# First tile of a time-mix and expert kernel: T1 to exponential in two halves, small constants on GpSimd, fourth tile's statistics in two pieces

## The reference, cut to what matters

```
xn  = layernorm(x);  xn1 = layernorm(xn) * ln1_g + ln1_b
r   = sigmoid(xn1 Wr');  w = -exp(xn1 Ww');  k = xn1 Wk';  v = xn1 Wv'
e   = exp(w + k);  decay = exp(time_decay)
num = decay*num + e*v;  den = decay*den + e      (a scan over the tokens)
a   = xn + (r * num / (den + 1e-8)) Wo'
a   = a + sigmoid(an Wrec') * (relu(an Wkey')^2 Wval'),   an = layernorm(a)*ln2_g + ln2_b
x2  = x + a
out = x2 + shared_ffn(h) + expert_ffn(h * score),   h = layernorm(x2), one expert of 16 per token
```

## Time and profile before

| what | value |
| --- | --- |
| median of 3 runs | 484.36 us (484.09 to 484.52) |
| the profiled execution's own time | 484.58 us |
| its span | 482.9 us |
| PE busy | 472.7 us (98%) |
| DVE busy | 371.4 us (77%) |
| POOL busy | 352.6 us (73%) |
| ACT busy | 324.2 us (67%) |
| moved by DMA | 39.32 MB, mean 81 GB/s |
| chain that ended last, by engine | PE 84%, DVE 6%, issue 3%, DMA 2%, ACT 2%, POOL 2% |

### The profile page before, as it was taken

How to read it: one execution, slowest core, us unless ns; L and a number is a source line. 1 busy time by engine, 2 the same in 40 slices (tenths; PEclk the granted TensorE clock), 3 DMA queues, 4 the chain that set the end, 5 groups by cost and what they waited for, 6 DMA issues and landing times.

```text
span 482.9 us, 10368 instructions
## 1 busy us (share of the span) xinstructions
PE 472.7 (98%) x3025; PEld 383.6 (79%) x3025; DVE 371.4 (77%) x1076; ACT 324.2 (67%) x625; POOL 352.6 (73%) x571
## 2 busy tenths in 40 slices
PE   8999999999999999999999999999999999999997
PEld 7556677868777778686777868877889999999996
DVE  7899899999999999996899989847545455555426
ACT  2777887987978879777687986563265555565421
POOL 6667498898898988986798877767326777767750
PEclk9999999999999999999999999999999999999999
DMA  7052001102102011010101001011489855542028
GB/s 240 2 191 115 1 23 44 56 12 67 34 33 68 23 45 56 12 66 24 44 24 46 33 12 46 33 42 39 121 187 246 229 167 150 150 130 72 23 68 282
DMA packets 33031, 39.32 MB, mean 81 GB/s; under 512 B 4913, under 2 KB 29113, under 8 KB 32720
## 3 DMA queue, kind: packets, MB, share of 16 engines
q1 hardware_dynamic: 26640, 24.98, 18.1%
q0 software_dynamic: 5760, 13.16, 7.8%
q10 hardware_dynamic: 576, 0.52, 0.3%
HBM read 21.69 MB, written 17.93 MB: 82 GB/s over the span
## 4 chain that ended last, share of the span: by engine, by line
PE 84%; DVE 6%; issue 3%; DMA 2%; ACT 2%; POOL 2%; SPq 1%; DVEq 0%; POOLq 0%; ACTq 0%
PE bank L442 20%; PE bank L435 11%; PE bank L459 6%; PE bank L450 4%; PE bank L850 4%; PE bank L858 3%; PE bank L857 3%; PE bank L548 3%; PE bank L560 3%; PE bank L544 3%; PE bank L539 3%; PE bank L429 3%; PE bank L534 2%; PE bank L605 2%; PE bank L619 2%
## 5 line engine op out<-in xcount | busy, mean ns | idle before, releaser
L442 PE MATMUL bank<-hT,wm 128*128 128x256 f32 x512 | 124.7, 383 | 0.6 <-ACT kr L974 0.6
L442 PEld LDWEIGHTS bank<-hT,wm 128*128 128x128 f32 x512 | 92.0, 190 | 18.7 <-issue 8.5
L1630 POOL DMA_INDIRECT sorted_rows<-rows,posi x64 | 72.8, 1138 | 20.1 <-issue 16.9
L1725 POOL DMA_INDIRECT out<-shared x55 | 53.2, 967 | 36.2 <-DVE shared L1542 22.7
L435 PEld LDWEIGHTS bank<-wm,k 128*128 128x128 f32 x512 | 61.7, 192 | 8.0 <-issue 6.4
L435 PE MATMUL bank<-wm,k 128*128 128x128 f32 x512 | 62.4, 275 | 0.1
L1153 ACT ACTIVATE er<-bank 128x256 f32<-128x256 f32 x40 | 15.3, 383 | 41.6 <-PE bank L858 40.9
L1550 DVE TENSOR_TENSOR e<-er,bank 128x256 f32<-128x256 f32 x40 | 16.8, 421 | 22.5 <-ACT er L1153 18.9
L459 PE MATMUL bank<-wm,actA 128*128 128x128 f32 x240 | 32.9, 280 | 0.0
L1010 ACT ACTIVATE h<-rows,smE 128x128 f32<-128x128 f32 x64 | 26.3, 482 | 8.1 <-POOL smE L1606 8.0
L459 PEld LDWEIGHTS bank<-wm,actA 128*128 128x128 f32 x240 | 29.3, 192 | 0.2 <-issue 0.2
(11 more groups left out here) (267 smaller groups left out, 1289.5 us busy)
## 6 DMA issues: line engine op xcount, KB each, us to landing
shared<-sorted_rows SPq DMA_DIRECT2D x56, 128.5 KB, 3.4
shared<-x SPq DMA_DIRECT2D x16, 256.0 KB, 2.8
rows<-sorted_rows SPq DMA_DIRECT2D x24, 128.5 KB, 2.4
wexp<-w_exp SPq DMA_DIRECT2D x2, 1536.0 KB, 8.6
sorted_rows<-filler SPq DMA_DIRECT2D x17, 128.5 KB
shared<-out SPq DMA_DIRECT2D x6, 256.0 KB
out<-shared SPq DMA_DIRECT2D x12, 128.0 KB, 2.2
sorted_rows<-rows,posi POOLq DMA_INDIRECT x64
```

The costliest lines, as they stand in the source:

```text
L442: ins = mm(dst[:, j * HALF:(j + 1) * HALF], W(name, 2 * pair_ + j), src[:, half * HALF:(half + 1) * HALF], start=True, stop=True)
L1630: g_.indirect_dma_start(sorted_ap, bass.IndirectOffsetOnAxis(posi[t % 3][:, g:g + 1].bitcast(U32), 0), rows[t % 3][:, g, :], None).then_in ...
L1725: g_.indirect_dma_start(out, bass.IndirectOffsetOnAxis(xr[k % RING][:, j, D:D + 1].bitcast(U32), 0), xr[k % RING][:, j, D + 1:ROW], None, ...
```

## The change

- Tile 0 goes from the transposes to the exponential in two halves of 256 tokens. PE transposes groups 0 and 1 into T1_B and groups 2 and 3 into T2_B, each half with its own wait. The Ww and Wk products are issued half by half (W, K, W, K), each half into a bank of its own. ACT copies, and takes both exponentials, half by half, and DVE subtracts half by half. The semaphores T1, xn1T, Wp, Kp, ew, z and e now count two for each tile; other tiles raise them by two at once.
- In the normalisation of tile 0, DVE now does groups 0, 1 and 3 (with a signal of its own behind group 1) and ACT group 2.
- `consts` and `rev_const` leave DVE. POOL does them right behind `col_no`, ahead of the powers of tile 0: five memsets, then `region0`, `region`, `part_row0`, `part_eid` and four pieces of `rev`. DVE waits for them (`const_p` at 8) behind the second piece of the statistics.
- The statistics of tile 3 leave the place ahead of DVE's rounds. Their first piece (`spread_of_x`, four BATCH_NORM_STATS2) stands between the two half subtractions, the second (`mean_of_x`, four BATCH_NORM_AGGREGATE) behind them.

```diff
-    agA=2, pA=3, xn1tok=1, xn0=1, T1=1, xn1T=1, Wp=1, Kp=1, Rp=1, Vp=1, ew=1, z=1, e=1, er1=2, ev=1,
+    agA=2, pA=3, xn1tok=1, xn0=1, T1=2, xn1T=2, Wp=2, Kp=2, Rp=1, Vp=1, ew=2, z=2, e=2, er1=2, ev=1,
...
+T1_of, W_of, K_of = (T1_B, T2_B), (W_B[:, 0:HALF], SMALL[:, 0:HALF]), (K_B[:, 0:HALF], T2_B[:, 0:HALF])
...
-HALF_TILE = 5
+HALF_TILE, CONSTS_P, ACT_GROUP = 5, 8, 2
...
     def transposes(dst, src, done):
...
-        ins.then_inc(s[done], 1)
+        ins.then_inc(s[done], PER[done])
...
-        if t == 0:
-            pe.wait_ge(s["const_d"], HALF_TILE)
...
+    def first_turn():
+        for half in range(2):
+            pe.wait_ge(s["const_d"], HALF_TILE + half)
+            if half:
+                wait(pe, "xn1tok", 0)
+            for g in range(2 * half, 2 * half + 2):
+                ins = nc.tensor.transpose(grp(T1_of[half], g), grp(xn1tok[0], g), ident[:, :])
+            ins.then_inc(s["T1"], 1)
+    def first_products():
+        pe.wait_ge(s["w_in0"], 16)
+        for half in range(2):
+            tokens = xn1T[0][:, half * HALF:(half + 1) * HALF]
+            wait(pe, "xn1T", 0, half + 1)
+            mm(W_of[half], W("Ww"), tokens, start=True, stop=True).then_inc(s["Wp"], 1)
+            mm(K_of[half], W("Wk"), tokens, start=True, stop=True).then_inc(s["Kp"], 1)
     def w_product(t):
-        pe.wait_ge(s["xn1T"], t + 1)
-        if t == 0:
-            pe.wait_ge(s["w_in0"], 16)
+        pe.wait_ge(s["xn1T"], 2 * (t + 1))
...
-        mm(W_B[:, :], W("Ww"), xn1T[t % 2][:, :], start=True, stop=True).then_inc(s["Wp"], 1)
+        mm(W_B[:, :], W("Ww"), xn1T[t % 2][:, :], start=True, stop=True).then_inc(s["Wp"], 2)
     def r_product(t):
-        pe.wait_ge(s["xn1T"], t + 1)
+        pe.wait_ge(s["xn1T"], 2 * (t + 1))
...
-            if t != 2:
+            if t == 0:
+                first_turn()
+            elif t != 2:
...
-            if t != 2:
+            if t == 0:
+                first_products()
+            elif t != 2:
...
+            if t == 0:
+                continue
...
-            mm(K_B[:, :], W("Wk"), xn1T[t % 2][:, :], start=True, stop=True).then_inc(s["Kp"], 1)
+            mm(K_B[:, :], W("Wk"), xn1T[t % 2][:, :], start=True, stop=True).then_inc(s["Kp"], 2)
...
     def norm_x(t):
...
-        for g in range(G if t else 1):
+        for g in range(G) if t else [ACT_GROUP]:
...
     def copy_x(t):
-        act_e.wait_ge(s["T1"], t + 1)
-        af(xn1T[t % 2][:, :], T1_B[:, :], ACT.Identity, bias=V("b1"), scale=V("g1")).then_inc(s["xn1T"], 1)
+        if t == 0:
+            for half in range(2):
+                part = slice(half * HALF, (half + 1) * HALF)
+                wait(act_e, "T1", t, half + 1)
+                af(xn1T[0][:, part], T1_of[half][:, part], ACT.Identity, bias=V("b1"), scale=V("g1")).then_inc(s["xn1T"], 1)
+            return
+        act_e.wait_ge(s["T1"], 2 * (t + 1))
+        af(xn1T[t % 2][:, :], T1_B[:, :], ACT.Identity, bias=V("b1"), scale=V("g1")).then_inc(s["xn1T"], 2)
...
     def exp_z(t):
+        if t == 0:
+            for half in range(2):
+                part = slice(half * HALF, (half + 1) * HALF)
+                wait(act_e, "z", t, half + 1)
+                af(e[0][:, part], ew[0][:, part], ACT.Exp).then_inc(s["e"], 1)
+            return
...
-        af(e[t % 2][:, :], ew[t % 2][:, :], ACT.Exp).then_inc(s["e"], 1)
+        af(e[t % 2][:, :], ew[t % 2][:, :], ACT.Exp).then_inc(s["e"], 2)
...
     def exp_w(t):
+        if t == 0:
+            for half in range(2):
+                wait(act_e, "Wp", t, half + 1)
+                af(ew[0][:, half * HALF:(half + 1) * HALF], W_of[half], ACT.Exp).then_inc(s["ew"], 1)
+            return
...
-        af(ew[t % 2][:, :], W_B[:, :], ACT.Exp).then_inc(s["ew"], 1)
+        af(ew[t % 2][:, :], W_B[:, :], ACT.Exp).then_inc(s["ew"], 2)
...
-    def consts():
-        for j in range(PACK):
-            ins = v.memset(place16[:, :, j], float(NE ** j))
-        const(ins)
-        dve.wait_ge(s["const_p"], 6)
-        const(v.tensor_scalar(region0[:, :], col_no[:, :], float(REGION), None, ALU.mult))
-        const(v.tensor_copy(region[:, :], region0[:, :]))
-        const(v.tensor_scalar(part_row0[:, :], col_no[:, :], float(REGION // P - 1), float(-FILL_ROW // P), ALU.mult, ALU.add))
-        const(v.tensor_scalar(part_eid[:, :], col_no[:, :], float(-NE), None, ALU.add))
     def half_tile():
...
-        for g in range(1, G):
+        for g in (0, 1, 3):
...
+            if g == 1:
+                nconst[0] += 1
+                ins.then_inc(s["const_d"], 1)
...
     def decay_const():
...
-    def rev_const():
-        for g in range(G):
-            ins = v.tensor_scalar(rev[:, g, :], col_no[:, :], -1.0, float(NE), ALU.mult, ALU.add)
-        const(ins)
...
     def stats_of_x(t):
+        spread_of_x(t)
+        mean_of_x(t)
+    def spread_of_x(t):
...
+    def mean_of_x(t):
...
     def k_less_w(t):
...
-        v.tensor_tensor(ew[t % 2][:, :], K_B[:, :], ew[t % 2][:, :], ALU.subtract).then_inc(s["z"], 1)
+        v.tensor_tensor(ew[t % 2][:, :], K_B[:, :], ew[t % 2][:, :], ALU.subtract).then_inc(s["z"], 2)
+    def first_k_less_w(half):
+        part = slice(half * HALF, (half + 1) * HALF)
+        wait(dve, "Kp", 0, half + 1)
+        wait(dve, "ew", 0, half + 1)
+        v.tensor_tensor(ew[0][:, part], K_of[half], ew[0][:, part], ALU.subtract).then_inc(s["z"], 1)
...
-            if t != 1:
+            if t == 0:
+                first_k_less_w(0)
+                spread_of_x(3)
+                first_k_less_w(1)
+                mean_of_x(3)
+                dve.wait_ge(s["const_p"], CONSTS_P)
+            elif t != 1:
...
-            if t == 0:
-                rev_const()
...
-    consts()
-    stats_of_x(3)
...
+    assert np_[0] == 6
+    for j in range(PACK):
+        g_.memset(place16[:, :, j], float(NE ** j))
+    const(g_.tensor_scalar(region0[:, :], col_no[:, :], float(REGION), 0.0, ALU.mult, ALU.add))
+    g_.tensor_copy(region[:, :], region0[:, :])
+    g_.tensor_scalar(part_row0[:, :], col_no[:, :], float(REGION // P - 1), float(-FILL_ROW // P), ALU.mult, ALU.add)
+    g_.tensor_scalar(part_eid[:, :], col_no[:, :], 1.0, float(-NE), ALU.mult, ALU.add)
+    for g in range(G):
+        ins = g_.tensor_scalar(rev[:, g, :], col_no[:, :], -1.0, float(NE), ALU.mult, ALU.add)
+    const(ins)
+    assert np_[0] == CONSTS_P
```

## The result

The change is slower: 485.60 us (median of 11 runs, 484.62 to 486.62) against 484.42 (11 runs, 484.09 to 484.67) of the kernel before, ratio 1.0026 with a 95% interval of 1.0017 to 1.0034. That is 1.2 us more where 0.53 less was forecast. The profiled execution took 486.44 us, its span is 484.6.

The account below looks back on a forecast made before the run. Tile 0's chain, mostly through DVE until PE takes over at 34.86 us, was taken to set when PE's long busy stretch begins. The scan 0.53 us earlier gave 484.36 - 0.53 = 483.83 us, range 483.0 to 484.9.

Parts of the forecast that it names:

- The start: Tile 0, transposes to DVE's scan: halves and moved constants bring the scan to 12.30 from 12.83, 0.53 us earlier.
- The first Ww pass: Tile 0 on PE: first half of the Ww product at about 9.12, without the idle 0.17 us.
- The second difference: Tile 0 on DVE: second half of k - exp(w) starts at about 11.35, directly behind tile 3's four statistics.
- PE's 24 passes: Where PE takes over the chain: they come at about 34.3 us for 34.86.
- POOL's power: POOL, ahead of tile 0: constants put its start at 5.4 to 5.9 us, 0 to 0.5 late, just hidden.
- The transposes at 7.7: PE, tile 0: transposes still start at about 7.7 us, held by the warm matmuls, not the normalised groups.
- such a wait as a sign of being wrong: Tile 0 on PE: the forecast is wrong if the transposes wait; no size given.
- Nothing new gets late. No later wait is changed: other tiles raise their semaphores by two in one step.: Behind tile 0's scan: partners come forward too, and counting by two adds no cost.
- A: Rival at tile 0 on DVE: all 1.03 us of freed constants count, giving 482.8 us; chance 0.15.
- B: Rival behind the first tile: a transfer or ACT's tile 1 work takes up the shift, 484.4 us; chance 0.15.
- C: Rival on ACT and DVE: four more short operations cost 0.69 us if none is hidden, 484.5 us; chance 0.08.
- D: Rival on POOL at the start: DVE's work stretches four constants, power 4.1 us late, 487.4 us; chance 0.07.

Follow-up runs that it names:

- e3: The change run once more, unaltered, for a second trace: 485.73 us (one run).
- e10: e1 with DVE's constants, `rev` and tile 3's statistics back on DVE as before, so the halves alone: 484.27 us (one run).
- e1: The change without counting by two: tile 0's first halves signal on idle semaphores, every tile raises by one; 484.22 us, ratio 0.9997 to before.
- e4: The kernel before run once more, unaltered, for a second trace: 484.82 us (one run).
- e6: e1 with 30 more waits on ACT, on a semaphore raised long ago: 484.26 us, ratio 1.0000 to before.
- e15: The change once more, timed beside e14: 486.44 us, ratio 1.0037 to before.
- e11: The kernel before with the small constants made by POOL as in the change, nothing else: 485.62 us (one run).
- e9: e1 with 12 warm matmuls for 16, six POOL constants moved to its third round and `rev` ahead of tile 1's wait for `num`: 484.49 us.
- e2: The kernel before with only the change's counting by two added: 488.36 us, ratio 1.0078 to before.
- e14: The change with 240 more waits on PE, from the fifth tile on, on a semaphore raised long before: 484.75 us, ratio 1.0000 to before.

## Why the prediction was wrong, by its own steps

**The start: right.** From transposes to scan 4.62 was forecast (12.30 less 7.68), 4.64 came. The first Ww pass was to come 1.44 behind the transposes without the idle 0.17, and came 1.33 behind (9.69 less 8.36), without it. The second difference was to start directly behind four statistics, and does (12.04). PE's 24 passes of 34.86 were forecast for about 34.3; e3, whose transposes are at 7.64, has them at 34.37:

```profile
24.63 1.22 DVE den L1462
...
34.37 2.94 PE bank L436 x24
```

**POOL's power: right.** 5.4 to 5.9 was forecast, 5.71 it is; eight operations 0.27 apart for 0.26, the memsets at about half the bound (0.31 for 0.55).

**The transposes at 7.7: right in the middle, with a spread that the prediction left out.** They start at 7.50 to 8.38 over the profiles with 16 warm matmuls, and at 7.43 in e10. Where the clock's record begins at 6.0 us or later the warm matmuls hold them, with no idle time ahead. Where it begins earlier (e1, e4, e6, e15) the warm matmuls are over before 7.5, and PE waits for the normalised groups until 7.50 (7.75 in e4). The prediction named such a wait as a sign of being wrong; e1, which has it, has no loss. This chance was not in the range, and both kernels have it.

**The step that failed: "Nothing new gets late. No later wait is changed: other tiles raise their semaphores by two in one step."** The waits' meaning was unchanged, their form wasn't. 28 of them became instructions of PE; the fetches of its code moved; at 315 us a fetch met the last packets of a scatter whose landing POOL waits for (3.64 for 1.74, 1.2 us on PE), and a 26th fetch fell into the last stores in some executions (1.3 us between e15 and e1). The prediction costed the counting at nothing without naming a resource that pays for an instruction. The queue of the code was on the page, and a share of 0.4% made it look like nothing.

**The same step, at the end of the kernel.** Without the counting by two the forecast would still have come out too fast: e1 has the gain at the start and is 0.13 us below before (484.22 against 484.35, a difference that can't be told from none), not 0.53. Its last addition on DVE is 1.2 us earlier than before's and its end only 0.6: between the two it takes 3.69 us, where before takes 3.11. The halves don't do this: e10, which has the halves alone, takes 3.15 there, and e11, which has POOL's constants alone, 3.89. What goes with the longer end is a piece on q14, the queue of the other engines' code. In before, e4 and e10 it starts 1.5 to 1.7 us ahead of the last addition, and the end takes 3.11 to 3.15. In the eleven traces with the constants off DVE and no piece of PE's code behind the last addition, it starts between 0.55 ahead and 1.95 behind, and the end takes 3.55 to 3.92. With the constants, DVE's records went from 1486 to 1474 and POOL's from 773 to 786. The data moved over the end of e10 and of e1 (40 slices of 478 to 484 and of 478 to 485 us) shows how: the stores of e10 stop at once, and those of e1 run out over three slices at 29, 23 and 18 GB/s, about what one of the 16 DMA engines moves (390 / 16 = 24, an estimate from the full slices):

```profile
GB/s 27 0 225 403 239 75 369 362 82 314 369 239 355 369 390 382 389 376 369 382 362 96 341 389 116 0 0 0 0 0 0 0 0 0 0 0 0 0 0 0
```

```profile
GB/s 310 322 88 334 304 287 363 112 117 380 386 375 375 380 375 404 229 29 23 18 0 0 0 0 0 0 0 0 0 0 0 0 0 0 0 0 0 0 0 0
```

So the constants' move, too, was costed at nothing behind the first tile, and the traces put some 0.6 us there. No run moved this piece alone; that it is the cause is read from where it lies in the traces, and not tested.

**The rivals.** A (freed time counts in full): e11 shows that the constants' move by itself is worth 0.1 to 0.3 and not 1.03. B (nothing arrives): no, PE's shift of 0.7 in e1 (0.72 at 15 us, 0.68 at 320) holds from 15 to 340 us. C (the fixed part of short operations): no, the halves' extra passes lie in idle time; ACT's 256-column passes took the 0.38 of the earlier trace rows. By the rule of the Trainium skill, Advanced Engine Details and Errata, section "The Read-Write Bubble", short operations cost more, and the rows agree on that price; it wasn't on the path. D (POOL slow) was the only rival on the right side and named the wrong cause at this place: the eight operations at 3.5 to 5.6 us were not stretched. In e9 POOL's operations beside DVE's `q` and its scan are (`region` 0.64 us for 0.20, the copy of the row numbers 1.12 for 0.19). The Trainium skill, SBUF — State Buffer, section "Who interferes with whom", says that a DVE instruction with two SBUF inputs contends with a GpSimd one that reads SBUF; e9's rows agree.

**What stays open.** Whether the q14 piece causes the longer end, and whose code it is: 31 more waits on ACT leave it in place (0.55 us ahead of the last addition in e1 and in the change), so it is hardly ACT's. Between 340 and 360 us PE's lead in e1 over before grows from 0.7 to 1.2; e6, which differs from e1 by ACT's waits alone, falls 0.35 behind it at the same place, so this is more likely the spread of executions than a gain. The counting by two delays PE by another 0.16 to 0.19 us at 43 us, in all five traces that have it (the change three times, e2, e14), and it wasn't tried why. No version here is measurably faster than the kernel before.

## What to carry to other kernels

Count the instructions that an edit adds to an engine or takes from it, waits included, for the longest engine above all, and look where the code fetches fall before and after: a semaphore that rises by two in place of one can turn a free wait into an instruction. Before an idea is dropped because its time came out wrong, separate it from its bookkeeping: here the halves gave at the start what was forecast, and the counting took more than that. And a difference of about 1 us in a kernel with fetches in the middle of its transfers can be undone or doubled by instructions that do nothing, so an edit of that size wants its trace compared at the far end as well as where it was made.

## What the runs showed of the hardware that was not expected

- PE's code comes by DMA during the kernel, in pieces of 16 KB for each 256 or so instructions, each 0.9 to 2.4 us of one DMA engine over all traces. In five traces a piece fell among the last packets of a scatter: the next packet started as the piece ended, to within 0.02 us, and the scatter landed 1.5 to 2 us later (POOL idle for 3.18 to 3.64 us, for 1.53 to 1.74 in the others).
- The other engines' code comes in pieces of 8 KB on a queue of its own, 30 of them here.
- A record of a wait can hold two semaphores: 240 waits added on PE made 120 records (e14). On semaphores raised long before, they cost PE 0.17 us in all (e14 against the change, up to 318 us: 0.33 ahead at first and 0.16 from 68 us on), where they don't move a fetch to a bad place.
- TensorE's clock rose between 5.05 and 8.03 us in executions of kernels that start alike, with PE busy from 1.90 on in all of them; the 16 warm matmuls were over between about 7.0 and 8.4 us accordingly.
